# Expert layer of a Mamba/MoE block on eight cores: the first four w2 chunks of an output group are cast behind, instead of ahead of, the eviction of the group before

## What is computed

```python
xn = _layernorm(x, axis=-1)
x = x + _L0_attn_ref(xn, ...) + _L0_ffn_ref(xn, ...)

def _L0_ffn_ref(hidden_states, router_w, router_b, w1, w2):   # E = 8, DIM = 1024, FFN = 4096
    logits = x @ router_w + router_b
    route = jax.nn.softmax(logits, axis=1)
    max_prob = jnp.max(route, axis=1, keepdims=True)
    max_ind = jnp.argmax(route, axis=1)
    for e in range(num_experts):
        h = x @ w1[e]
        a, g = jnp.split(h, 2, axis=1)
        y = jax.nn.silu(a) * g @ w2[e]
        out = jnp.where((max_ind == e)[:, None], y, out)
    out = out * max_prob
```

## Time and profile before

| What | us |
|---|---|
| median of three runs | 8689.67 |
| the runs | 8297.27, 8689.67, 9191.67 |
| profiled execution | 8200.54 |
| its span on the slowest core (core 3) | 8199.0 |
| spans of the eight cores | 8102.9 to 8199.0 |
| TensorE busy on core 3 | 6636.0 (81%) |
| VectorE busy on core 3 | 3246.8 (40%) |

### The profile page before, as it was taken

How to read it: one execution, slowest core, us unless ns; L and a number is a source line. 1 busy time by engine, 2 the same in 40 slices (tenths; PEclk the granted TensorE clock), 3 DMA queues, 4 the chain that set the end, 5 groups by cost and what they waited for, 6 DMA issues and landing times.

```text
span 8199.0 us, 90986 instructions; the slowest of 8 cores (8102.9 to 8199.0 us)
## 1 busy us (share of the span) xinstructions
PE 6636.0 (81%) x28776; PEld 2858.7 (35%) x28776; DVE 3246.8 (40%) x6770; ACT 1677.6 (20%) x1615; POOL 65.7 (1%) x130
## 2 busy tenths in 40 slices
PE   4545459899999999999754454699999999999998
PEld 1112114344444444444321121244443444444343
DVE  3443533434334343333334434333334343333333
ACT  1313213122131312213032131222131212213030
POOL 0000000000000000000000000000000000000000
PEclk9569569999999999999885785899999999999797
DMA  4114024444444444444440130344444444444343
GB/s 130 47 39 146 1 69 140 144 136 152 133 155 134 140 146 131 154 133 155 134 144 3 69 116 1 109 134 155 131 157 131 139 147 133 155 133 145 113 143 102
DMA packets 408969, 979.76 MB, mean 119 GB/s; under 512 B 47584, under 2 KB 310016, under 8 KB 338880
## 3 DMA queue, kind: packets, MB, share of 16 engines
q1 hardware_dynamic: 400896, 956.48, 35.9%
q0 software_dynamic: 7616, 17.46, 0.7%
HBM read 965.10 MB, written 8.39 MB: 119 GB/s over the span
## 4 chain that ended last, share of the span: by engine, by line
PE 72%; DVE 12%; issue 6%; DMA 5%; ACT 3%; DVEq 2%; ACTq 1%; POOL 0%; SPq 0%; POOLq 0%
PE p_fa L1127 21%; PE p_fg L1137 21%; PE p_fo L1229 20%; DVE acc L1290 2%; PE p_w L922 2%; DVE tmp L1286 2%; PE p_sb L633 2%; PE p_z L411 1%; PE p_z L335 1%; DMA stg<-w1t 1%; DMA stg<-wgate 1%; DMA stgw<-w2t 1%; ACT L667 1%; PE pY L795 1%; PE p_cv L358 1%
## 5 line engine op out<-in xcount | busy, mean ns | idle before, releaser
L1229 PE MATMUL p_fo<-A,w2bf 128*128 128x512 bf16 x8192 | 1912.4, 399 | 279.3 <-DVE w2bf L1196 279.3
L1127 PE MATMUL p_fa<-xn,wbf 128*128 128x512 bf16 x8192 | 1875.8, 383 | 25.9 <-DVE wbf L1112 25.1
L1137 PE MATMUL p_fg<-xn,wbf 128*128 128x512 bf16 x8192 | 1871.8, 382 | 0.0
L1149 ACT ACT_TABLE_LOAD x512 | 656.9, 1283 | 4334.2 <-PE p_fa L1127 4334.2
L1082 DVE TENSOR_TENSOR A<-wbf,p_fg 128x1024 bf16<-128x1024 bf16 x512 | 624.9, 1220 | 2183.6 <-PE p_fg L1137 2183.6
L1229 PEld LDWEIGHTS p_fo<-A,w2bf 128*128 128x128 bf16 x8192 | 829.5, 102 | 1359.8 <-issue 569.5
L1127 PEld LDWEIGHTS p_fa<-xn,wbf 128*128 128x128 bf16 x8192 | 805.7, 99 | 1015.0 <-issue 106.6
L1137 PEld LDWEIGHTS p_fg<-xn,wbf 128*128 128x128 bf16 x8192 | 806.3, 98 | 981.5 <-issue 64.6
L1196 DVE CAST w2bf<-stgw 128x256 bf16<-128x256 f32 x2048 | 587.7, 293 | 1199.2 <-PE p_fo L1229 880.7
L1112 DVE CAST wbf<-stg 128x2048 bf16<-128x2048 f32 x484 | 593.8, 1227 | 51.6 <-DVE A L1082 2.7
L1149 ACT ACTIVATE wbf<-p_fa 128x1024 bf16<-128x1024 f32 x512 | 524.3, 1024 | 5.7
(11 more groups left out here) (145 smaller groups left out, 2479.2 us busy)
## 6 DMA issues: line engine op xcount, KB each, us to landing
stg<-w1t SPq DMA_DIRECT2D x512, 1024.0 KB, 4.8
stgw<-w2t SPq DMA_DIRECT2D x2048, 128.0 KB, 2.2
stg<-win_x SPq DMA_DIRECT2D x64, 768.0 KB, 4.9
stg<-wgate SPq DMA_DIRECT2D x64, 512.0 KB, 4.3
stg<-wout SPq DMA_DIRECT2D x32, 1024.0 KB, 5.8
stg<-win_b SPq DMA_DIRECT2D x32, 512.0 KB, 3.8
stg<-win_c SPq DMA_DIRECT2D x32, 512.0 KB, 3.8
acc<-u_t POOLq DMA_DIRECT2D x16, 512.0 KB, 10.5
```

The source lines that it names most:

```text
L1127: ins = t.matmul(p_fa[p][:, tsl * 512:(tsl + 1) * 512], wbf[:, p * 2048 + k * 128: p * 2048 + (k + 1) * 128], xn[:, k * HT + tsl * 512: k ...
L1137: ins = t.matmul(p_fg[p][:, tsl * 512:(tsl + 1) * 512], wbf[:, p * 2048 + 1024 + k * 128: p * 2048 + 1024 + (k + 1) * 128], xn[:, k * HT + ...
L1149: ins = s.activation(wbf[:, p * 2048: p * 2048 + 1024], p_fa[p][:, :], AF.Silu)
L1229: ins = t.matmul(p_fo[gp_par * 4 + o2 * 2 + tsl][:, :], w2bf[:, s4 * 256 + o2 * 128: s4 * 256 + (o2 + 1) * 128], A1[:, j * HT + tsl * 512: ...
```

## The change

The advance chunks of groups 1 to 3 are no longer emitted at the end of the group before. They are emitted at the start of their own group, with the same guards (`prev_cast[28 + j]`, `prev_mmlist[28 + j]`), and so behind the eviction `f_v2` and, after group 2, behind the w1 prefetch. Only for group 0 of the next expert they are still emitted at the end of group 3, ahead of the eviction. No instruction is added or removed.

```diff
                         if og == 0 and pend_w2 is not None:
                             w2_dma = list(pend_w2[0])
                             w2_cast = list(pend_w2[1])
-                        elif og > 0 and state.get("w2_pend_next"):
-                            w2_dma = list(state["w2_pend_next"][0])
-                            w2_cast = list(state["w2_pend_next"][1])
-                            state["w2_pend_next"] = None
                         else:
                             w2_dma, w2_cast = [], []
...
                             elif j < 4:
-                                emit_w2_dc(j, e, og, w2_dma, w2_cast,
-                                           state["prev_w2_cast"],
-                                           state["prev_ffn_mm"] if og == 0 else None)
+                                if og == 0:
+                                    emit_w2_dc(j, e, og, w2_dma, w2_cast,
+                                               state["prev_w2_cast"],
+                                               state["prev_ffn_mm"])
+                                else:
+                                    emit_w2_dc(j, e, og, w2_dma, w2_cast,
+                                               prev_cast[28 + j],
+                                               prev_mmlist[28 + j])
...
                         prev_cast = w2_cast
-                        nxt = None
-                        if og < 3:
-                            nxt = (e, og + 1)
-                        elif e < NE - 1:
-                            nxt = (e + 1, 0)
-                        if nxt is not None:
+                        prev_mmlist = w2_mm
+                        if og == 3 and e < NE - 1:
                             n_dma, n_cast = [], []
                             for jn in range(4):
-                                emit_w2_dc(jn, nxt[0], nxt[1], n_dma, n_cast,
+                                emit_w2_dc(jn, e + 1, 0, n_dma, n_cast,
                                            w2_cast[28 + jn], w2_mm[28 + jn])
-                            if og < 3:
-                                state["w2_pend_next"] = (n_dma, n_cast)
-                            else:
-                                state["w2_pend"] = (n_dma, n_cast)
+                            state["w2_pend"] = (n_dma, n_cast)
```

## The result

The changed kernel takes 1.0185 times as long as before, with a 95% interval of 1.0146 to 1.0224: slower beyond doubt, and on either side of 2% by its interval. A die time is the median span of the four cores of a die; its median over the runs is 8110 us before and 8256 with the change, +146 us or 1.8%.

The account below looks back on a forecast made before the run. TensorE, busy 81%, was taken to bound the kernel, waiting in the w2 pass for casts late in VectorE's order. Terms 114 + 27 + 0 = 141 us gave ratio 1.0172, carried to 8839 us; range 8360 to 9080.

Parts of the forecast that it names:

- D: Rival: the four casts ahead of the eviction cover nothing and order is indifferent, 0 to -7 us; chance 0.04.
- Plain borders: 34 group borders without w1 prefetch: four chunks uncovered, eviction 0.21 us earlier, 3.24 us each; with 4 us for lower clock, 114.
- Chunk 4's load covered: At plain borders, chunk 4's later-issued load still lands about 1 us before its matmuls are due: 0 us, at most 34.
- The clock: After longer plain gaps TensorE's clock falls more, losing 2.3 us per piece instead of 1.5: 27 us, bounds 0 and 44.
- Prefetch borders: 14 borders with w1 prefetch: loads issued 3.45 us earlier offset 3.45 us of uncovered matmuls; 0 net, bounds -50 to +48 us.
- A: Rival: early w1 loads win nothing, so the 14 prefetch borders lose their covered chunks too; 189 us, 2.3%; chance 0.20.
- B: Rival: early w1 loads land before the last matmul of group 2 and leave the chain; 91 us, 1.1%; chance 0.13.
- Rival C: More gaps let TensorE draw less, so the late lower-clock stretch goes, up to 90 us back; 51 us, 0.6%; chance 0.06.

Follow-up runs that it names:

- e4: The changed kernel with 28 thrown-away matmuls added at each of 32 plain borders, before the wait for the first cast; ratio 1.0084 to the kernel before, die 8182 us.
- e2: The kernel before with the new order at the 14 borders with the w1 prefetch only; ratio 0.9991, die 8109 us.
- e3: The changed kernel with the two w1 loads kept behind the four w2 loads on the sync queue; ratio 1.0232 to the kernel before, die 8303 us.
- e1: The kernel before with the new order at the 34 plain borders only; ratio 1.0165, die 8249 us.
- e8: The changed kernel with the advance chunks of the next expert's group 0 not emitted in advance either; die 8301 us, no ratio.
- e9: The kernel before with the eviction of groups 0 to 2 in four parts and w1 loads spread as eight of 256 KB; ratio 0.9628, die 7808 us.
- e7: The kernel before with w1 casts moved late into group 3 and the eviction of groups 0 to 2 in four parts; die 7849 us, no ratio.

## Why the prediction was right and where it was wrong

The call was wrong: "the same" had a chance of 0.62 and "slower" 0.35, and the kernel is slower. The sum behind the call was right, 141 us where the die has 146 and core 5 has 153, and so was the mechanism. The ratio was forecast as 1.0172 and measured as 1.0185.

The step that failed is the last one, from the sum to the chances: "About 2% is what a measurement of this kernel can tell from no change; the sum is just below". No row stood behind these 2%. The three runs then shown, 8297 to 9192 us, differ by far more, and the spans of the four cores of die 1 by far less (8102.9 to 8123.1). What the runs showed in its place: the die time of the kernel before repeats between 8101 and 8129 us, and the 95% interval of the ratio is 0.8% wide, 1.0146 to 1.0224, so that a loss of 1.7% is told from none with ease. Of the mechanisms in the list only D, at 0 to -7 us, had no loss; all others had 0.6% or more. The answer that follows from the sum is "slower", by 1.7%.

The terms, measured where nothing else is said on core 5, before and after:

- Plain borders, 34 x 3.24 us and 4 us for the stretch at the lower clock, 114. Right in kind, a little small. The gaps grew from 3.66 to 7.11 us on average, by the whole 3.45 us of the four chunks, 117 us. (On core 1 TensorE's idle time at the w2 matmuls is 399.8 us, where 390 was forecast.) The 0.21 us that an earlier eviction was to give back did not show: on core 1 it starts 0.18 us after the modelled end of the last matmul where I had taken 0.11, and TensorE resumes 6.83 us behind that instead of 6.71; for the rest of the difference between 6.8 and 7.1 us I have no row. The 4 us belong to the profiled execution of core 3 and are no part of what core 5 shows.
- Chunk 4's load covered, 0 us. Right, but with less to spare than the 1 us that I had. On core 1 the cast of chunk 4 waits 2.52 us for its load and ends at 1863.43; its matmuls are due at 1860.00 + 3.45 = 1863.45 at the full clock, and later at the clock that was granted there, 0.50. In e4, at the full clock, the piece runs without a stall.
- The clock, 34 x (2.3 - 1.5) = 27 us. Right in kind, too small. The average loss of a piece behind a plain gap was 1.51 us and became 2.48, 33 us; with the prefetch borders (2.24 to 2.51) it is the 36 us by which the w2 matmuls took longer. The clock fell at every plain border: no piece behind a gap of 7 us takes 27.79 us, on core 5 or on core 1.
- Prefetch borders, 0. Right, and shown by e2 (0.9991) and e3 (47 us more when the SP order alone is undone). The 14 gaps average 10.47 us, before 10.48; on core 1 after and core 3 before 11.03 and 11.02. Rivals A and B, which moved this term to either end, both fell.
- Rival C, that the stretch at the lower clock goes, isn't borne out: the changed kernel's profile has one too, with a granted clock of 0.80 from 2235 to 2262 us on core 1, and core 5, which has none before or after, is slower by the whole 153 us. D fell with e1.

That the time, 8931 us in the median of all runs, lies in the stated range of 8360 to 9080 is luck. The forecast of 8839 rested on a median before of 8690, the ten runs before have 8438, and between 8438 and 8931 lie 5.8%, of which the change explains 1.8.

## What to carry to other kernels

Where one engine both prepares operands and clears results, the order in its queue is the schedule: put the operands that the next stage needs first ahead of the clearing, and cut the clearing into pieces that fit between further preparations. Here four casts ahead of an eviction were worth 1.8%, and cutting the eviction as well another 2.9%. Count what a moved block issues on every queue, since a load moved up may pay for a cast moved back; and look at what becomes late when a wait goes.

## What was not expected of the hardware

Work that is thrown away made the changed kernel faster (8182 us against 8256; the kernel before has 8110): 28 extra matmuls in each of 32 gaps took 74 us off. The granted clock stayed at the 2.4 GHz level through gaps of 1 us (128 matmuls in 27.79 us behind 31 of 32) and fell in each of those of 7 us. In between it went either way: behind gaps of 3.6 to 4.8 us 7 of 29 pieces on core 3 of the kernel before were at full speed, and behind the gaps of 2 us in e8 3 of 14.

Large loads delay small ones behind them on the same queue by more than I had allowed: casts of 128 KB chunks, whose loads land 2.2 us after issue in the median, waited 4.06 us when 2 MB stood ahead. With the 2 MB cut into 256 KB loads among them, in e9, one cast of core 1 waited more than 3 us (3.08), against 15 on core 5 of e7.
